# Constant products in TensorE's waits: the expert prologues and attention's lead

## The reference, cut to what matters

```
x = x + 0.5 * experts(layernorm(x))      # 8 experts, each token goes to its best 2
x = x + attention(layernorm(x))          # 16 heads of 16, causal, 512 tokens a sequence
x = x + 0.5 * experts(layernorm(x))      # the same experts again
x = x + 0.5 * hadamard_ffn(layernorm(x))
x = x + feature_attention(layernorm(x))
x = x + 0.5 * hadamard_ffn(layernorm(x))

experts:  logits = x @ gate_w.T + gate_b; top 2 by softmax
          h = x @ w1[e].T + b1[e]; y = glu * sigmoid(1.702 * glu) * (lin + 1)
          out += (y @ w2[e].T + b2[e]) * weight
```

## Time and profile before

| | |
|---|---|
| median of 3 runs | 1249.7 us (1246.36 to 1256.46) |
| the profiled execution | 1244.61 us, span 1242.7 us |
| mean granted clock of TensorE | 0.886 |
| PE busy | 1034.4 us (83%) |
| PEld (weight loads) busy | 840.2 us (68%) |
| VectorE (DVE) busy | 742.2 us (60%) |
| ScalarE (ACT) busy | 461.3 us (37%) |
| GpSimd (POOL) busy | 443.4 us (36%) |

### The profile page before, as it was taken

How to read it: one execution, slowest core, us unless ns; L and a number is a source line. 1 busy time by engine, 2 the same in 40 slices (tenths; PEclk the granted TensorE clock), 3 DMA queues, 4 the chain that set the end, 5 groups by cost and what they waited for, 6 DMA issues and landing times. The chain is left out here.

```text
span 1242.7 us, 18068 instructions
## 1 busy us (share of the span) xinstructions
PE 1034.4 (83%) x6196; PEld 840.2 (68%) x6196; DVE 742.2 (60%) x1761; ACT 461.3 (37%) x804; POOL 443.4 (36%) x474
## 2 busy tenths in 40 slices
PE   4469993589999998353799974999989999789997
PEld 2358882456565755233678874888878888678886
DVE  6844443877687774168454445556646767666554
ACT  3314331346666666033243321222324433222322
POOL 2036654325444422021366520000137879500000
PEclk9579997678999999665899996999976999999999
DMA  9023223100000000370242242000010030000001
GB/s 341 1 60 111 85 85 124 61 1 1 2 1 18 1 19 17 85 273 9 68 167 88 82 139 70 1 1 1 1 68 1 1 69 1 1 1 17 18 8 27
DMA packets 38524, 66.03 MB, mean 53 GB/s; under 512 B 8195, under 2 KB 29732, under 8 KB 38054
## 3 DMA queue, kind: packets, MB, share of 16 engines
q1 hardware_dynamic: 30758, 43.90, 11.0%
q0 software_dynamic: 7680, 20.98, 5.2%
HBM read 43.89 MB, written 20.97 MB: 52 GB/s over the span
## 5 line engine op out<-in xcount | busy, mean ns | idle before, releaser
L1752 PE MATMUL ps<-xt,w 128*128 128x512 f32 x768 | 193.8, 402 | 5.6 <-PEq L66 3.2
L1752 PEld LDWEIGHTS ps<-xt,w 128*128 128x128 f32 x768 | 142.7, 192 | 37.0 <-DVE xt L136 6.2
L1501 DVE CUSTOM_DVE_ANT_0 ps<-ps,att_mask 128x128 f32<-128x128 f32 (+3 forms) x256 | 119.0, 516 | 37.9 <-PE ps L1153 37.7
L571 PE MATMUL ps<-moe_w,moe_narrow_xb 128*128 x480 | 127.0, 401 | 0.0
L468 POOL DMA_INDIRECT moe_xs<-xn_rows,moe_index x80 | 81.1, 1013 | 127.5 <-DVE moe_index L848 84.3
L1848 DVE TENSOR_TENSOR had_gated<-ps,had_sig 128x512 f32<-128x512 f32 x64 | 44.3, 692 | 119.2 <-ACT had_sig L1805 119.2
L102 POOL TENSOR_TENSOR var_eps<-bn,eps 128x4 f32<-128x4 f32 x24 | 5.4, 227 | 296.6 <-DVE bn L96 296.6
L474 POOL DMA_INDIRECT made_rows<-moe_units_made,moe_index x80 | 81.1, 1014 | 77.0 <-ACT moe_units_made L681 64.8
L1805 ACT ACTIVATE had_sig<-ps 128x512 f32<-128x512 f32 x64 | 38.3, 598 | 186.0 <-PE ps L1752 186.0
L571 PEld LDWEIGHTS ps<-moe_w,moe_narrow_xb 128*128 128x128 f32 x480 | 92.6, 193 | 19.1
L865 DVE TENSOR_TENSOR moe_narrow_xb<-ps,moe_narrow_xb 128x512 fp32r<-128x512 f32 x40 | 27.7, 692 | 128.9 <-ACT moe_narrow_xb L663 128.9
(11 more groups left out here) (254 smaller groups left out, 2262.1 us busy)
## 6 DMA issues: line engine op xcount, KB each, us to landing
moe_w<-in_moe SPq DMA_DIRECT2D x16, 768.0 KB, 8.7
xn_rows<-moe_wide_xn SPq DMA_DIRECT2D x8, 512.0 KB, 9.4
back<-made_rows SPq DMA_DIRECT2D x8, 512.0 KB, 5.3
x<-x_turned SPq DMA_DIRECT2D x8, 512.0 KB, 7.8
moe_w<-made_rows SPq DMA_DIRECT2D x8, 512.0 KB, 4.9
x<-in_x SPq DMA_DIRECT2D x4, 512.0 KB, 5.3
x_turned<-x SPq DMA_DIRECT2D x4, 512.0 KB, 2.9
moe_narrow_later<-in_w SPq DMA_DIRECT2D x4, 512.0 KB, 3.3
```

The lines of the kernel that those rows point to most:

```text
L571: last = nc.tensor.matmul(h_bank(j, i), xb[a][:, j % 2, i, k, :], weight(c), start=False, stop=(k == KC - 1 and c == 1))
L1501: last = nc.vector.tensor_tensor_reduce(g.ps[:, a, col:col + n], g.ps[:, a, col:col + n], mask[:, SEQ - n:SEQ], -1.0, 3.0e38, ALU.add, ALU ...
L1752: last = nc.tensor.matmul(g.ps[:, bank(n, half), :], w[a][:, k, c * P:(c + 1) * P], xt[low][:, b % 2, k, :], start=(k == 0 and q == 0), st ...
```

## The change

A helper `spin` issues `count` products of `ident` and `column` into a PSUM bank; nothing reads what they write. It is called at seven places of TensorE's list, each behind a wait: in each expert prologue 13 and 13 products between the counts and the slot products, and 10, 13 and 6 between the slot products and the first `turn`; in attention's lead 26 products when batch 0's rows are loaded, and 10 each when the second and the third tile are split. The other engines' lists stay as they are.

```diff
+def spin(nc, g, bank, count):
+
+    for _ in range(count):
+        nc.tensor.matmul(g.ps[:, bank, 0:P], g.ident[:, :], g.column[:, :], start=True, stop=True)
...
             nc.tensor.matmul(g.ps[:, 3, 0:TILES * E], g.strict[:, :], by_expert, start=True, stop=True) \
                 .then_inc(ranked, 1)
+            spin(nc, g, 4, 13)
+            pe.wait_ge(routed, 16)
+            spin(nc, g, 4, 13)
             for r in range(2):
                 pe.wait_ge(spread, r + 1)
...
             last.then_inc(tokens_ps, 1)
 
+            pe.wait_ge(index_done, 1)
+            spin(nc, g, 4, 10)
+            pe.wait_ge(owner_done, 1)
+            spin(nc, g, 4, 13)
+            pe.wait_ge(lo_split, E - 2)
+            spin(nc, g, 4, 6)
             pe.wait_ge(lo_split, E)
...
+            pe.wait_ge(g.back_here[0], 32)
+            spin(nc, g, 0, 26)
             turn_x(0, 0, 0)
             turn_x(0, 1, 1)
...
+            for i in (2, 3):
+                pe.wait_ge(lo_done, i)
+                spin(nc, g, 0, 10)
             turn_q1(0)
             turn_k(0)
```

## The result

| | before | after |
|---|---|---|
| median of 22 runs each | 1251.73 us | 1242.58 us |
| lowest and highest | 1242.42 to 1258.88 | 1226.87 to 1253.27 |
| profiled execution | 1244.61 us | 1246.89 us |
| its mean granted clock | 0.886 | 0.903 |

The ratio is 0.9906, with a 95% interval of 0.9879 to 0.9932: faster by 11.8 us (0.0094 x 1251.7; 8.5 to 15.1). The medians lie 9.2 us apart. The ratio leaves out nine of the 22 runs of after as slow, all of them above 1245.5 us, and none of before's; over all 22 and 22 runs the means lie 8.5 us apart, with a 95% interval of 5.2 to 11.8. The profiled execution of before happened to be among its shorter ones and that of after among its longer ones, so the two traces are compared stretch by stretch and not by their spans.

A forecast was written before the change was run, and what follows sets the result against it. VectorE was taken to bound the expert prologues, TensorE the stretch behind, VectorE and GpSimd attention's lead. Stage gains of 3.2 and 3.3 us, the lead 0, made 6.5 off the median 1249.7: 1243.2 us, range 1236 to 1250.

The forecast's parts named there:

- First set: Expert prologue, 26 products before the slot products: they end ahead of these, and VectorE's L835 moves 1.57 us earlier.
- Second set: Expert prologue, 29 products before the first `turn`: 9.1 us, overrunning the splits by 0.9, leaving 0.7 of the 1.57 us.
- the term of 5 us at 1.2 GHz: Each added set: the clock rises after 5 us at 1.2 GHz; lower bound 3.2 us, upper bound never.
- First pair: Expert stage, first `turn` and product group run at full clock: 0.5 us and 1.97 us gained.
- Each stage: Gain of an expert stage: 3.2 us in the first, 3.3 in the second, carried whole because TensorE bounds what follows.
- The lead's 26 products: Attention's lead: an even chance that the clock lasts to the first projection; 0.8 us gained, bounds 0 and 2.0.
- The rule on transposes: Attention's lead: transposes do not count toward full clock, so the projection runs cold; the term is 0.3 us, not 0.8.
- The tens: Attention's lead, 10 and 10 products before `turn_q1`: half of a possible delay counted, a loss of 0.7 us (0 to 1.6).
- The lead as a whole: Attention's lead: gains and losses net 0.1 us, called 0, from -1.6 to +2.0.
- Rival (a): Clock also holds through attention's lead and into the step loop: 1237 to 1239 us, down to 1236; chance 0.17.
- Rival (b): Clock falls before the real work, or the second set overruns too far: 0 to 3 us won, 1247 to 1250; chance 0.23.
- Rival (c): Products overrun the waits, chiefly the prologue's second set, the clock never rising: slower, 1259 us; chance 0.05.

The follow-up runs named there:

- bridged: The changed kernel without the 10 and 10 products, plus 8 products between attention's first transposes and its first projection: 1241.22 us, ratio 0.9914.
- 8 columns: The changed kernel with all 156 added products kept in place but 8 moving columns each instead of 128: 1283.04 us, ratio 1.0154.
- the gates' products: The bridged kernel plus 10 products in the gates' wait of each prologue and 11 and 8 around the Hadamard stage's first transposes: 1232.8 us, ratio 0.9858.

## Why the prediction was right, and where its sum was short

The forecast was 6.5 us. Measured were 11.8 (8.5 to 15.1) by the ratio, 9.2 by the medians and 8.5 (5.2 to 11.8) by the means of all runs. The time lies in the range, and "within 1%" is what happened, by little. That the forecast of 1243.2 us lies only 0.6 from the median of 1242.58 is partly luck: the median of three runs that it started from was 2.0 below the later one of 22, and this cancelled most of what the gain was short by. The mechanism of the prologues was right at each step; the size was short.

- **First set.** Predicted to take 8.4 us, measured 8.73 (the clock came at 50.35, 5.7 us into it and not 5). L850 stopped waiting, and the 1.57 us came. Right.
- **Second set, the step that was mis-sized.** The prediction took 9.1 us with 5 us at 1.2 GHz, an overrun of 0.9, and kept 0.7 of the 1.57. Measured: 8.22 us, an overrun of 0.1 (VectorE's last split ends at 69.00), all of the 1.57 and 0.1 more. The working itself was good: alone, behind cold slot products, the set took 9.11 us. What failed is the term of 5 us at 1.2 GHz for a set that follows the first one. It holds for the second set alone (start at 63.08, clock back at 68.09). With the first set ahead, the clock is up from 50.35 to 57.2, falls there, and is back at 64.0, 3.1 us into the set. The prediction's own lower bound of 3.2 us gives 8.2, which is what came.
- **First pair.** Predicted 0.5 + 1.97 = 2.47; measured 7.82 - 5.40 = 2.42 in the first stage. Right.
- **Each stage.** 3.2 and 3.3 predicted; 4.1 and 4.2 by the second `turn`. At the last `turn` it is 4.9 and 5.0. That 0.8 more is one trace against one; the table's last `turn` differs by up to 3.3 us between kernels with the same prologue (137.71 in after, 140.98 bridged), so no cause is named for it. Whether it is real stays open.
- **The lead's 26 products.** Predicted 0.8 (0 to 2.0) on the ground that it was even whether the clock survives to the projection. It fell in three of four executions; where it held, the lead was 2.4 us shorter, and 2.8 with the bridge, beyond the bound. The bound was too low ahead of the projection: it put 0.2 to 0.3 there, but where the clock held, the projection started 0.8 us earlier (11.94 against 12.72 behind the first `add_back`), of which the transposes' earlier start is 0.3; VectorE's wait then fell from 2.50 to 1.04, by 1.5 where 1.6 to 1.8 were counted. What the bounds left out on the other side is that a clock that comes back later makes the second projection cold too, 0.7 us in after.
- **The rule on transposes**, "TensorE: Matmul & The Clock Gate" of the Trainium skill, section "Part 4: PE-mode transpose", gave 0.3 for this term. Three falls in four speak for it more than the even chance did. But the gap held some 3 us of idleness too (1.42 + 1.91 in after), and once the clock held across the transposes, so the runs don't tell a transpose from an idle engine here.
- **The tens.** Predicted a loss of 0.7 (0 to 1.6), with `turn_q1` behind the products and a cold second ten. Measured 0.4 to 0.7 in four traces, in just that way. The size is right partly by luck: the prediction priced a cold second ten at 1.2 to 1.6 and took half of it as an even chance, and the second ten were mostly cold in all four. They made `turn_q1` 1.4 to 1.7 us late and not 2.1, and VectorE's addition hid 0.8 to 1.1 of that.
- **The lead as a whole.** 0 predicted, between -1.6 and +2.0; measured -0.6 to +1.4 with tens and no bridge, in three traces; the four leads with no products in them take 35.7 to 36.3 us.
- **Against the rivals.** Rival (a) asked that the clock hold through the lead and into the loop. It did not; the part of it that came true is the 1.57 and 0.5 and 2.0 in each stage, its first sum of 8.2. Rival (b), 0 to 3 us, is excluded by the interval and by the 4.1 and 4.2 us at the second `turn`. Rival (c) came to pass only with 8 columns.

The account of what is shown: 8.3 us by the second `turn` of the two stages, nothing from the lead. The means of all runs give 8.5, so nothing need be missing. The 11.8 of the ratio would leave up to 3.5 us without a cause; the 0.8 in each expert loop, if it is real, would be 1.6 of them.

## What to carry to other kernels

Where an engine's clock depends on what it has just done, fill a wait only if real work of that engine follows within a short gap, and size the products so that they end with the wait, neither behind it (the tens, 8 columns) nor long ahead of it (the first set with the gates' products before it, whose end moved from 0.8 to 1.7 us ahead of the slot products). A delay of the filled engine costs only what the next engine isn't busy with anyway: `turn_q1` came 1.4 to 1.7 us late and `out_k` 0.4 to 0.7. Price each fill from rows at both clocks, and price the fill that follows from the clock that the one before leaves. Compare stretches between fixed instructions, as two whole traces of a kernel with a scattering clock differ by more than the edit is worth.

## What the runs showed of the hardware

- The added float32 products took 0.215 us a pass with 8 moving columns and 0.21 with 128, both at 1.2 GHz. With 8 columns PE was busy for 11.10 of 11.10 us and the clock stayed at 0.50; with 128, in the bridged lead, the products start at 206.81, and the clock is 0.50 up to 211.00 and 1.00 from 212.00. A PE that shows as busy was no sign of a rising clock here.
- The clock in attention's loop falls at places that differ between executions, 22.7 to 53.8 us in all, and the loop takes 226.95 to 238.13 us. That is more than this change is worth.
- The expert loop took 113 to 117 us from its second `turn` to its last on two chips and 106 to 111 on the others, with the same durations of products and, in the trace shown, with late gathers. Why those chips' gathers are late is not shown.
